# Row maxima of the attention scores: one VectorE reduction for each score chunk in place of two for every short one, and one product in place of four per half of the heads

## The reference

```python
h = jnp.swapaxes((x @ W1 + b1).reshape(B, S, H, 3 * d), 1, 2)
q, k, v = (h[..., :d], h[..., d:2 * d], h[..., 2 * d:])
w = jnp.einsum('bhqd,bhkd->bhqk', q, k) / dk
mask = jnp.tril(jnp.ones((S, S), dtype=x.dtype))
w = softmax(w * mask - (1.0 - mask) * 1e6, axis=-1)
a = einsum('bhqk,bhkd->bhqd', w, v)             # then  a @ Wp + bp
x = layernorm(x + attention)
xr, xk = mu * x + (1 - mu) * x_prev             # one mu each
out = sigmoid(xr @ W_r.T) * (relu(xk @ W_k.T) ** 2 @ W_v.T)
x = layernorm(x + out)
```

## Time and profile before

| | |
|---|---|
| median of 3 runs | 714.41 us (711.55 to 716.44) |
| the profiled execution | 715.99 us, its span 714.3 us |
| PE busy | 84% |
| DVE busy | 74% |
| ACT busy | 65% |
| POOL busy | 61% |
| mean granted clock of PE | 0.944 |

### The profile page before, as it was taken

The page is one execution under the profiler, slowest core; times in us unless marked ns, Lnnn a source line. Parts: engine busy times, 40 slices in busy tenths (PEclk is TensorE's granted clock), DMA queues, the critical chain, the costliest instruction groups (busy, mean ns, idle before and its releaser), DMA issues.

```text
span 714.3 us, 19231 instructions
## 1 busy us (share of the span) xinstructions
PE 599.9 (84%) x7405; PEld 321.4 (45%) x7405; DVE 530.4 (74%) x1388; ACT 464.6 (65%) x918; POOL 439.0 (61%) x680
## 2 busy tenths in 40 slices
PE   2359997999999999998989999899999998988623
PEld 1025453545454545454545454454545454533311
DVE  3058887889898888888898989797988888832121
ACT  1210776686878787778687777778687767676410
POOL 6110434467677676868676858576767767667653
PEclk9995899999999999999999999999999999989655
DMA  1332323132322323232323232415142332000100
GB/s 56 86 94 89 106 65 108 44 120 49 97 86 66 118 62 122 62 121 62 121 55 121 52 112 62 109 46 135 48 104 79 66 102 64 18 17 17 31 15 15
DMA packets 63615, 53.63 MB, mean 75 GB/s; under 512 B 8730, under 2 KB 59292, under 8 KB 63524
## 3 DMA queue, kind: packets, MB, share of 16 engines
q1 hardware_dynamic: 63524, 52.41, 26.2%
HBM read 34.82 MB, written 17.30 MB: 73 GB/s over the span
## 4 chain that ended last, share of the span: by engine, by line
PE 35%; POOL 25%; DVE 13%; ACT 11%; issue 10%; DMA 3%; SPq 2%; POOLq 0%; DVEq 0%; ACTq 0%
PE ops L537 9%; PE sps L493 7%; POOL probs L777 6%; PE spare L399 6%; ACT probs L616 5%; DVE rowmax L687 5%; POOL rstd L799 4%; POOL h L804 4%; POOL result L804 4%; PE spare L413 3%; PE spare L407 3%; PE tps L473 2%; POOL step_d L811 2%; DVE qk_rest L715 2%; DVE stats L698 2%
## 5 line engine op out<-in xcount | busy, mean ns | idle before, releaser
L616 ACT ACTIVATE probs<-tps 128x512 f32<-128x512 f32 x640 | 341.7, 598 | 125.6 <-PE tps L473 125.4
L687 DVE TENSOR_REDUCE rowmax<-sps 128x1 f32<-128x512 f32 (+2 forms) x768 | 337.7, 503 | 53.8 <-PE sps L507 52.0
L777 POOL TENSOR_SCALAR_AFFINE_SELECT probs<-probs 128x512 f32<-128x512 f32 x256 | 157.7, 633 | 157.5 <-ACT probs L616 157.0
L493 PE MATMUL sps<-kop,qop 52*128 52x384 bf16 (+3 forms) x1024 | 220.2, 310 | 34.3 <-DMA kop<-d_parts 13.8
L473 PE MATMUL tps<-qop,kop 54*128 54x128 bf16 (+3 forms) x1024 | 219.5, 304 | 12.6 <-ACT probs L616 12.6
L537 PE MATMUL ops<-probs,vop 128*32 128x384 f32 (+3 forms) x2048 | 172.7, 444 | 8.7 <-POOL probs L777 6.3
L493 PEld LDWEIGHTS sps<-kop,qop 52*128 52x128 bf16 x1024 | 71.3, 95 | 158.3 <-DVE rowmax L687 86.5
L505 PE MATMUL sps<-qmask,rows_of 64*128 64x128 bf16 (+1 forms) x640 | 134.3, 212 | 0.0
L507 PE MATMUL sps<-qmask,rows_of 64*128 64x128 bf16 (+1 forms) x640 | 131.8, 208 | 0.0
L691 DVE TENSOR_REDUCE rowmax<-sps 128x2 f32<-128x512 f32 x128 | 79.5, 684 | 13.7 <-PE sps L507 12.7
L537 PEld LDWEIGHTS ops<-probs,vop 128*32 128x32 f32 x2048 | 55.3, 110 | 73.1 <-issue 46.0
(11 more groups left out here) (75 smaller groups left out, 650.0 us busy)
## 6 DMA issues: line engine op xcount, KB each, us to landing
d_parts<-qk_parts SPq DMA_DIRECT2D x16, 768.0 KB, 3.9
qop<-d_parts SPq DMA_DIRECT2D x192, 32.0 KB
qop<-d_parts SPq DMA_DIRECT2D x64, 96.0 KB
kop<-d_parts SPq DMA_DIRECT2D x192, 32.0 KB
kop<-d_parts SPq DMA_DIRECT2D x64, 96.0 KB
xa<-L_attn_x SPq DMA_DIRECT2D x16, 256.0 KB, 3.0
xres<-L_attn_x SPq DMA_DIRECT2D x16, 256.0 KB, 3.4
out<-result SPq DMA_DIRECT2D x16, 256.0 KB, 2.5
```

Of the source, the lines that this page charges most:

```text
L493: nc.tensor.matmul(sps[:, bank(n), off:off + w], qop[r, par, pair, BLK * a:BLK * a + BLK], kop[r, par, pair, 0:w], start=j == 0, stop=Fals ...
L616: nc.scalar.activation(probs[:, g % 2, i, :], tps[:, bank(4 * GROUPS * n + 4 * g + i), :], ACT.Exp, scale=SCALE)\
L687: last = nc.vector.reduce_max(rowmax[:, par, QUARTET * half + t, hh, a:a + 1], sps[:, bank(n), off:off + w], axis=AX_X)
L777: last = nc.gpsimd.affine_select(out=v, in_=v, compare_op=ALU.is_ge, fill=0.0, base=0, pattern=[[0, QUARTET], [1, BLK]], channel_multiplie ...
```

## The change

Every chunk is reduced by one instruction. A short chunk now holds query block 0 in its first 128 columns and query block 2 in the other 384, and one reduction gives four maxima, one for each 128 columns: that of block 0 and three partial ones of block 2. `rowmax` grows by a dimension of four for the partial maxima. Once per half, after chunk 1 of groups 4 and 9, one more instruction joins the three partial maxima of each of 8 heads; it waits for the reductions of the groups before, and `max0` and `max1` wait for it (`block2_done`). The product of the values with the inverse sums is one instruction per half in place of four. In the diff the empty lines are left as they are.

```diff
 def max_unit(u):
     if u < 2 * QUARTET:
         t, short = divmod(u, 2)
         if short:
-            return [(t, 2, 0, 3 * BLK), (t, 0, 3 * BLK, BLK)]
+            return [(t, 0, 0, BLK), (t, 2, BLK, 3 * BLK)]
         return [(t, 3, 0, SEQ)]
...
 def diagonals(ap, u):
     if u < 2 * QUARTET:
-        return ap[:, (2 if u % 2 else 3) * BLK:].rearrange("p (j w) -> p j w", w=BLK)
+        blocks = ap.rearrange("p (j w) -> p j w", w=BLK)
+        return blocks[:, 0:NQBLK:3] if u % 2 else blocks[:, 3:]
...
-        rowmax = sb("rowmax", [P, 2, PAIRS, 2, NQBLK])
+        rowmax = sb("rowmax", [P, 2, NQBLK, PAIRS, 2, NQBLK])
...
                 elif use == "max0":
                     wait(pe, s_reduced, 4 * GROUPS * before("S", b) + 2 * GROUPS)
+                    wait(pe, block2_done, 2 * before("S", b) + 1)
                     last = rowmax_transpose(1 - par, 0)
                 elif use == "max1":
                     wait(pe, s_reduced, 4 * GROUPS * (before("T", b) + 1))
+                    wait(pe, block2_done, 2 * (before("T", b) + 1))
                     last = rowmax_transpose(par, 1)
...
                 wait(dve, s_done, n + 1)
-                if u < 2 * QUARTET:
-                    for t, a, off, w in max_unit(u):
-                        last = nc.vector.reduce_max(rowmax[:, par, QUARTET * half + t, hh, a:a + 1],
-                                                    sps[:, bank(n), off:off + w], axis=AX_X)
+                pair = QUARTET * half + max_unit(u)[0][0]
+                if u >= 2 * QUARTET:
+                    last = nc.vector.reduce_max(rowmax[:, par, 0, pair:pair + 2, hh, 1],
+                                                sps[:, bank(n), :].rearrange("p (j w) -> p j w", j=2), axis=AX_X)
+                elif u % 2 == 0:
+                    last = nc.vector.reduce_max(rowmax[:, par, 0, pair, hh, 3:], sps[:, bank(n), :], axis=AX_X)
                 else:
-                    pair = QUARTET * half + max_unit(u)[0][0]
-                    last = nc.vector.reduce_max(rowmax[:, par, pair:pair + 2, hh, 1],
-                                                sps[:, bank(n), :].rearrange("p (j w) -> p j w", j=2), axis=AX_X)
+
+                    last = nc.vector.reduce_max(rowmax[:, par, :, pair, hh, 0],
+                                                sps[:, bank(n), :].rearrange("p (j w) -> p j w", w=BLK), axis=AX_X)
                 last.then_inc(s_reduced, 1)
+                if c == CHUNKS - 1 and i == 1:
+
+                    wait(dve, s_reduced, n - 1)
+                    of = rowmax[:, par, :, QUARTET * half:QUARTET * half + QUARTET].rearrange("p j t h a -> p a (t h) j")
+                    nc.vector.reduce_max(of[:, 2, :, 0], of[:, 0, :, 1:], axis=AX_X).then_inc(block2_done, 1)
...
-                    for t in range(TT):
-                        last = nc.vector.tensor_tensor(
-                            attn[:, t, DH * half:DH * half + DH].rearrange("q (r h) d -> q r h d", h=2),
-                            tiles[:, 0, t], inv[:, half, t].unsqueeze(3).to_broadcast([P, QUARTET, 2, DH]), ALU.mult)
-                    last.then_inc(spare_read, 1)
+                    nc.vector.tensor_tensor(
+                        attn[:, :, DH * half:DH * half + DH].rearrange("q t (r h) d -> q t r h d", h=2), tiles[:, 0],
+                        inv[:, half].unsqueeze(4).to_broadcast([P, TT, QUARTET, 2, DH]), ALU.mult).then_inc(spare_read, 1)
```

More of the change, by code:

```diff
@@ L232, in block_program @@
         s_reduced = sem("s_reduced")
+        block2_done = sem("block2_done")
         max_high = sem("max_high")
@@ L393, in rowmax_transpose @@
             def rowmax_transpose(par, half):
-                src = rowmax[:, par, QUARTET * half:QUARTET * half + QUARTET].rearrange("p t h a -> p (t h a)")
+                src = rowmax[:, par, 0, QUARTET * half:QUARTET * half + QUARTET].rearrange("p t h a -> p (t h a)")
                 return nc.tensor.transpose(spare[0:MAXIMA, 0:P], src, ident)
```

## The result

The changed kernel takes 715.94 us, the median of 20 runs (712.33 to 718.06). The kernel before, run beside it as often, takes 712.41. The ratio is 1.0043, with an interval of 1.0027 to 1.0058: 3.1 us more, between 1.9 and 4.1 (the medians differ by 3.5). The difference is within the 1% that I called no change, and the time is in the range and 1.4 us above the predicted 714.5; but it is clear of zero, where my sum had +0.1. The profiled execution took 716.62 us with a span of 714.9 us, against 715.99 and 714.3.

A forecast was written before the change was run, and what follows sets the result against it. A loop through POOL's run from masks to `step_d` was taken to bound the kernel, not VectorE. Terms -0.5 - 0.2 + 0.8 = +0.1 us gave 716.1 for the profiled execution, so 714.5 by the median; range 709.5 to 718.5.

The forecast's parts named there:

- my sum: Whole kernel: first steps -0.5, end product -0.2, order on PE +0.8, together +0.1 us, from -1.5 to +1.3.
- What bounds the kernel: Full steps: a loop through PE, ACT and POOL sets the pace, not VectorE's short-chunk reductions; freeing VectorE there gains nothing.
- The loop through POOL's run: Full step: PE (0, 3), groups 1 to 5, ACT group 6, POOL masks to `step_d`, `scaled`, exponential (0, 0), PE again.
- The idle weight loads: PE before stage S matmuls, 200 to 560 us: 46.7 us idle, released by maxima; taken as evidence for VectorE-bound rivals.
- Short chunks: VectorE's short-chunk reductions: 0.66 us becomes 0.60, freeing 0.06 us each, at most 0.14; worth nothing in full steps.
- the fourth rival: VectorE: reducing to four maxima costs as much as its pieces, 0 to +4 us, 716.5 or so; chance 0.05.
- Join and product: VectorE: join 0.1 us, nothing in full steps; one product takes 0.42 us, freeing 0.19, -0.2 us at the very end.
- The first steps: Stage S alone and next step's products, where PE waits for VectorE: -0.5 us, between 0 and -1.3.
- The order in a short chunk: PE at (0, 3): the 384-column piece behind the T matmul costs 0.06 us a step, 14 steps, +0.8 us (0 to +1.5).
- The weight load: PE's short chunks: the 384 columns' weight load no longer hides, up to 0.095 us each, 11 us, 726; chance 0.05.
- the mask rows: PE's two mask matmuls, each with its own weight load in the same rows, start 0.06 us apart: evidence the load hides.

The follow-up runs named there:

- r8: r4's kernel with `step_d` computed by VectorE at the head of group 9 in place of POOL; 708.06 us, ratio 0.9922 to the kernel before.
- r6: The changed kernel with the `xres` load issued ahead of the store and reload of the second half's maxima; 709.25 us, ratio 0.9970 to the kernel before.
- r7: The kernel before with the same earlier `xres` load on SyncE; 709.13 us, ratio 0.9959 to the kernel before.
- r1: The kernel before with only PE's order in a short chunk changed, 128 columns first and 384 second; 715.39 us, ratio 1.0021.
- r2: The changed kernel with the old order in a short chunk, 384 columns first; 715.79 us, ratio 1.0009 to the kernel before.
- r4: The changed kernel with all of stage S at chunk (0, 3) ahead of the T matmul on PE; 714.90 us, ratio 1.0013 to the kernel before.
- r5: The kernel before, unchanged and measured again as a control; 713.87 us, ratio 1.0023 to itself.
- r9: The kernel before with one more, long met, wait of PE at each of the two transposes of the maxima; 712.57 us, ratio 1.0004.
- r10: The kernel before with only the four products per half made one; 714.78 us, ratio 1.0028.
- r3: The changed kernel, unchanged and measured again; 717.40 us, ratio 1.0039 to the kernel before.

## Why the prediction was right, and what it missed

*What bounds the kernel.* Right. The loop through POOL's run held: `scaled` waited for `step_d` in 14 steps as before, VectorE's 18.1 us bought no full step a shorter period, and r8 moved the step by taking POOL's last link away. The idle weight loads of the earlier trace rows spoke for VectorE and were, as argued from chunk (0, 3), of no account.

*Short chunks.* Right: 0.60 us from start to start, 0.06 less than before, and four maxima for the price of one, which disposes of the fourth rival. The estimate from the Trainium skill ("VectorE: DVE Perf Modes", the TRN2 errata) was 0.125 us for each. This case's trace disagrees: 0.06 by the starts, and the two stretches of the first S step and the one after it gave 0.37 us together, where I had 0.3 by the rows (four short chunks less one join in each).

*Join and product.* Right: 0.10 and 0.42 us, and -0.2 at the end.

*The first steps.* Sized -0.5, measured -0.67: -0.37 from the reductions (0.3 in the sum) and -0.30 from the products.

*The order in a short chunk.* Right in place and size: +0.06 us a step, in 13 steps and not 14, +0.8 as foretold (+0.9 by r6 against r7). r1 brought it in alone, r2 and r4 took it out.

*The weight load.* The rival fell as the mask rows said it would: 332.90 and 332.96.

*What was missed.* The sum had no term for the first step with stage D, where the stored maxima must land before the `xres` load is issued. I had listed no DMA among the things that change. The mean of (4, 0) to (5, 0) is 5.69 us for old reductions (before, r1, r5, r9, r10) and 8.13 for new ones (after, r2, r3, r4, r8): +2.4 us. Of this 1.8 is PE's later start at line 541, 19.6 us after the step's first reduction against 17.7, and it goes with the landing (3.5 us against 1.7 in the mean). Some 0.15 is the fourth row's gain, waited away, and 0.5 the lower clock, which is chance at least in part. The sum becomes -0.67 - 0.2 + 0.8 + 2.4 = +2.3, and +3.1 (1.9 to 4.1) was measured.

The change itself thus lies outside the -1.5 to +1.3 that I gave the sum, and that the forecast held has luck in it. It started from 714.41 us, the median of three runs; twenty have 712.41, so a start that was 2.0 too high hid more than half of what the sum missed. And it stayed within 1% since the whole term is only a third of that; a term four times as large would have been missed just as well.

The chain from there on is shown: a later landing, a later `xres`, `xbias`, masks, and PE idle. PE also loses its clock in this stretch. The windows of the trace (start:end, length, busy time and count of PE, weight loads, DVE, ACT, POOL, then the granted clock, DMA share and GB/s) of after, then of before:

```profile
120.00:125.00 5.00, 0.57 (x10) 0.37 (x14) 1.78 (x4) 1.21 (x3) 2.62 (x4) 0.88 0.72 253
125.00:128.00 3.00, 3.00 (x25) 1.14 (x25) 0.51 (x1) 0.55 (x2) 0.99 (x2) 0.50 0.38 125
```

```profile
124.00:127.00 3.00, 3.00 (x29) 1.83 (x29) 1.29 (x2) 1.08 (x2) 1.05 (x2) 0.67 0.40 118
```

PE was busy 0.57 of 5 us, and in the next three it ran at 0.50, which is 1.2 GHz; in the kernel before the same stretch had 0.67. At the lower level the matmuls of line 541 take 1.94 us in place of 1.07. The time at half clock is 6.8 us in after, r2, r3, r5, r8 and r10 and 3.4 in before, r1, r4 and r9, so it doesn't plainly go with the change. What it costs is seen in four kernels with the same quick landing: the step takes 37.67 and 37.69 us in r1 and r9, 38.78 and 38.71 in r5 and r10, so 1.0 us of chance between executions. r6 and r7, without the idle time, have none, and their matmuls of this line take 1.07.

*Why the store lands late.* Five of its packets stand behind a transfer of instructions. These are the transfers (queue and kind, packets, MB, share of 16 engines) that start in after from 113.45 to 114.50 us, from 114.50 to 114.70 and from 115.90 to 116.20:

```profile
q1 hardware_dynamic: 75, 0.02, 8.8%
...
q8 instruction: 1, 0.02, 44.9%
...
q1 hardware_dynamic: 5, 0.00, 4.7%
```

And in r5 from 112.69 to 113.75 and from there to the reload at 114.09:

```profile
q1 hardware_dynamic: 80, 0.02, 9.3%
...
q8 instruction: 1, 0.02, 23.8%
```

The store is 80 small packets. In r5 all of them have ended 1.03 us after the issue, a packet of 16 KB of instructions begins behind them, and SyncE goes on after 1.40. In after 75 have ended by then; the packet of instructions runs from 1.10 to 2.54 us, the last five of the store start as it ends, and SyncE goes on after 3.63. Four later stores land after 2.4 to 3.4 us in every one of the 14 profiles, where the step around them is at most 0.3 us longer than its neighbours. With the one at this place that makes 70 stores. In all 64 of them that land after 2.4 to 3.7 us exactly five of 80 packets start as such a packet ends; in the six that land after 1.40, all of them at this place, none does. Five of 80 is what one of the 16 DMA engines would have, but the profile doesn't name a packet's engine.

*What stays open* is why the instructions get ahead of the five packets in all seven profiles of kernels with new reductions and in one of seven with old ones. The start of their packet doesn't part the two forms: 0.95 to 1.64 us after the issue in the late ones, 1.16 to 1.58 in the quick. PE's added wait alone doesn't do it (r9), nor the product alone (r10), nor the order on PE alone (r1, 1.39). What is left are the reductions with four maxima, the join, the four times larger `rowmax`, or several parts together, and I didn't part these.

The Trainium skill ("DMA: Bandwidth & Descriptors", the anatomy of one DMA, described for a transfer that GpSimd issues) puts most of a fixed cost of some 2 us down to the receipt of the write. This case's trace doesn't show that for SyncE's store: in the quick form 0.37 of 1.40 us lie behind the last packet, and 0.8 before the first.

## What to carry to other kernels

Idle time before a matmul with VectorE as its releaser is no evidence that VectorE bounds the loop: look at what stands behind that matmul in PE's order, here an exponential 1.07 us later. When the pieces of one matmul change places, look for the spot where the second piece stands behind another engine's wait; there the larger piece costs 0.06 us in every step. Don't read "lands late" as idle queues before the packets are looked at: a transfer of instructions, which no line of the kernel issues, stood in front of part of a small store here. And list the stores and loads between the edited instructions and their readers, one chain per stage that starts: a load that has no need of a round trip through memory should be issued ahead of it, which was worth some 3 us in the kernel before and 5 in the changed one, more than the whole change to VectorE.

## What the runs showed of the hardware that I had not expected

- A store of 16 KB was seen as landed after 1.4 us in six profiles and after 3.0 to 3.7 us in eight, at one place of the program. In the eight, five of its 80 packets waited for a packet of 16 KB of instructions to end.
- A tensor-tensor operation of VectorE with both inputs in SBUF slowed POOL beside it: two masks took 1.68 us, not 1.23, and VectorE took 1.15 for what it did in 0.70 in the last step of the same run, with no mask beside it. The Trainium skill ("GPSIMD Engine Reference", the table of specifications) says that POOL shares its SBUF interfaces with VectorE and contends with instructions of two SBUF inputs; the trace agrees, 0.45 us for one such operation.
- PE's idle stretch of 2.0 to 4.4 us in the first step with stage D costs twice: once as idle, and again as 3.4 to 6.8 us at half clock; the longer stretch costs 1.0 us more than the shorter. The kernels without it (r6, r7) kept the full clock there.
